# Contextual attention, two layers: half of the paste as fp16 products, three turning banks, chunks cut anew

## The chip, the cores and the metric

The kernel runs on one core of a Trainium2 chip. The metric is the device time of one execution in microseconds, lower is better; the number given is the median of three runs.

## The reference

Two equal layers, each over 4 images of 64 channels, 80 x 80, in fp32. For one image `b`:

```
f  = b[:, :, ::2, ::2]                                # 64 x 40 x 40
w  = 3x3 patches of f                                 # L = 1600 rows of 576
raw_w = 4x4 patches of b at stride 2                  # 1600 rows of 1024
wn = w / max(|w|, 1e-4)
y  = wn @ w.T * mm                                    # 1600 x 1600 scores
y  = softmax(10 * y, over the rows of wn) * mm
patches = y.T @ raw_w                                 # 1600 x 1024
out = patches added back where they overlap, / 4      # "paste", a transposed convolution
```

`mm` is 1 where the mask's 3x3 patch is all zero. Layer 2 takes layer 1's output. The 8 passes (2 layers x 4 images) are called units here.

## The kernel before, in words

The 40 x 40 points of `f` lie in 14 tiles of 123 (3 strips x 41). `G` holds the whole score matrix of a unit, 14 tiles of rows by 14 blocks of 123 columns. A unit goes through two stages, and the stages of two units lie side by side.

**Scores.** 28 score pairs (two tiles of rows each) in 4 column chunks (`S_CHUNKS`, start and width in blocks). PE's `score_tile` makes a tile's scores in `psG` (2 banks, one for each tile of a pair) with 14 fp16 matmuls over the split features `HL`, `LH`, `H1`, `HV` (L433); blocks that the symmetric matrix already holds are transposed out of `G` instead (fp32, L428), and then the first tile of the pair waits until ACT has copied all earlier tiles. DVE takes the scaled maximum (L723), ACT copies the scores to `G` (L565) and sums the exponentials (L575). At the end of a unit the log of the sum is made column by column (`lse_*`) and spread over rows by PE (`lse_row`, L362, into `psB`).

**Paste.** 28 paste pairs in 4 chunks (`P_CHUNKS`), each of two tiles. DVE turns scores into arguments (`argument_pair`, L773, one operand in PSUM), ACT takes the exponential (`softmax_pair`, L586), SP moves each tile down by one partition into `SH` (L270, four DMAs a pair), DVE adds it back (`add_shifted`, L784) and adds the neighbour tile into `Z` (`sum_pair`, L806, both operands in SBUF; `Z` has two slots of a pair). PE's `paste_tile` (L449) multiplies `Z` by the patch blocks `B` into `psO`, one bank for each of two column parities `b`; every fp32 matmul shows as two MATMUL records, so a tile has four. After 7 pairs ACT copies both banks out (`read_out`, L595) and SP stores them. The blocks `B` of the next unit are transposed by PE (`block_group`, L409) and copied by ACT (L549) one group a slot, in slots 21 to 27.

**The order** is written by hand. Each engine has a `body(u, v, w)`: unit `u` is pasted, `v` scored, `w` prepared, over slots `s` = 2 to 29; in a slot one pair of `u` is pasted and the score pairs of `score_list(s)` are made (PE: first score tile, first paste tile, second score tile, second paste tile). Slots 28 and 29 already paste chunk 0 of `v` and have no scores. `argument_pair` and `softmax_pair` run 4 slots ahead (`LEAD`), `add_shifted` 2 (`AHEAD`), `sum_pair` 1. In DVE's slot the order is argument, shifted add, sum, then scores; in ACT's: softmax, read_out (every 7 slots), scores, block group. At slot 24 `lse_row` of the first chunk stands on PE between the two halves. The body runs 9 times: once with scores alone, 7 times with both, once with paste alone. The features of the next unit are laid out by 8 DMAs on SP at slot 28 (L251), and POOL only copies a seam (`wrap`, L919, reads and writes `G`). Ahead of the first body DVE works out the mask and then `low_features(0)`, on which the first layout waits.

## Time and profile before

| | us |
|---|---|
| median of 3 runs | 1791.49 (1788.55 to 1794.37) |
| the profiled execution | 1782.45 |
| its span, first to last instruction | 1780.6 |
| PE, PE weight loads busy | 1591.8, 1052.2 |
| DVE, ACT, POOL busy | 1090.1, 901.4, 51.2 |
| mean granted TensorE clock | 0.952 |

The profile is of one execution. A busy time is the sum over an engine's instructions; matmuls overlap, so PE's real rate is read from the starts of successive groups, not from their lengths. In the rows below PE is the matmul engine, PEld its weight loads; "x9" is the number of instructions merged into a row, and the last bracket is the idle time ahead of it and what ended it. Busy times of a window stand in the order PE, PEld, DVE, ACT, POOL, then the granted clock.

### The profile page before, as it was taken

The numbers are of one execution on the slowest core, as the hardware profiler recorded it, in microseconds if no ns is written. First come the engines' busy times: TensorE is split into PE (matmuls) and PEld (weight loads), VectorE is DVE, ScalarE is ACT, GpSimd is POOL, SyncE is SP. The second block draws the span as 40 slices with busy tenths as digits, with TensorE's granted clock in tenths as the row PEclk, the third lists the DMA queues.
The fourth block names the chain that finished last, engine by engine and source line by source line (L and its number), as shares of the span: only waits on it lengthen the run. The fifth ranks groups of instructions, "written<-read, shape, count | busy, mean of one in ns | idle before, by whom it ended". The sixth has DMA issues, their size and how long they took to land.

```text
span 1780.6 us, 27285 instructions
## 1 busy us (share of the span) xinstructions
PE 1591.8 (89%) x7260; PEld 1052.2 (59%) x7260; DVE 1090.1 (61%) x2526; ACT 901.4 (51%) x2265; POOL 51.2 (3%) x62
## 2 busy tenths in 40 slices
PE   3887899998999899998999989999899989999986
PEld 3756566665666566565665656666566656656543
DVE  5224555675566756576656755667556676667784
ACT  1446454574446744565535645457344573457431
POOL 1000100001000000000000010000100000000100
PEclk9987899999999999998999999999889999999998
DMA  3400624226422445225352262422633234522342
GB/s 61 62 1 12 143 61 89 72 70 139 84 63 72 104 111 106 55 69 124 86 96 61 66 145 66 92 72 73 137 71 77 72 94 109 106 64 66 112 122 78
DMA packets 181701, 149.64 MB, mean 84 GB/s; under 512 B 120016, under 2 KB 177424, under 8 KB 181520
## 3 DMA queue, kind: packets, MB, share of 16 engines
q1 hardware_dynamic: 181522, 147.62, 35.1%
q8 instruction: 67, 1.10, 0.3%
q14 instruction: 112, 0.92, 0.2%
HBM read 19.78 MB, written 13.11 MB: 18 GB/s over the span
## 4 chain that ended last, share of the span: by engine, by line
PE 71%; DVE 10%; ACT 8%; issue 7%; SPq 2%; DMA 1%; DVEq 0%; ACTq 0%; POOL 0%; POOLq 0%
PE psG L433 35%; PE psO L449 30%; DVE S L723 4%; ACT S L575 3%; PE psG L428 3%; DVE G L773 2%; PE psM L347 2%; ACT G L565 2%; ACT OSB L595 1%; ACT G L586 1%; PE psB L362 1%; SPq L251 1%; DVE Z L806 1%; DVE G L784 1%; ACT SQ L529 1%
## 5 line engine op out<-in xcount | busy, mean ns | idle before, releaser
L449 PE MATMUL psO<-Z,B 123*128 123x492 f32 (+2 forms) x1792 | 786.5, 569 | 66.7 <-ACT OSB L595 57.9
L723 DVE CUSTOM_DVE_ANT_0 S<-psG,RB 123x369 f32<-123x369 f32 (+1 forms) x448 | 267.4, 605 | 547.3 <-PE psG L433 471.0
L565 ACT ACTIVATE G<-psG 123x369 f32<-123x369 f32 (+1 forms) x448 | 236.6, 529 | 695.8 <-DVE mx L723 693.9
L449 PEld LDWEIGHTS psO<-Z,B 123*128 123x128 f32 x1792 | 335.9, 199 | 301.3 <-issue 202.3
L433 PE MATMUL psG<-LH,HL 128*123 128x369 f16 (+3 forms) x2592 | 474.8, 329 | 26.2 <-issue 13.8
L433 PEld LDWEIGHTS psG<-LH,HL 128*123 128x123 f16 x2592 | 338.0, 138 | 175.3 <-issue 94.9
L586 ACT ACTIVATE G<-G,nb 123x492 f32<-123x492 f32 (+1 forms) x448 | 268.2, 646 | 125.5 <-DVE G L773 125.1
L575 ACT ACTIVATE S<-S,nm 123x360 f32<-123x360 f32 (+3 forms) x560 | 306.3, 551 | 0.1
L773 DVE SCALAR_TENSOR_TENSOR G<-G,RA,psB 123x492 f32<-123x492 f32 (+1 forms) x448 | 275.4, 658 | 21.8 <-issue 18.2
L784 DVE TENSOR_TENSOR G<-G,SH 123x492 f32<-123x492 f32 (+1 forms) x448 | 251.2, 601 | 14.7 <-DMA SH<-G 14.5
L806 DVE TENSOR_TENSOR Z<-G 123x984 f32<-123x984 f32 (+2 forms) x192 | 209.8, 1093 | 30.4 <-PE psO L449 30.3
L433 PE MATMUL psG<-H 128*123 128x369 f16 (+3 forms) x864 | 187.8, 327 | 0.0
L428 PEld LDWEIGHTS psG<-idn,G 123*123 123x123 f32 x688 | 103.8, 206 | 106.9 <-ACT G L565 81.9
L428 PE MATMUL psG<-idn,G 123*123 123x123 f32 x688 | 124.2, 302 | 43.0 <-ACT G L565 42.4
L433 PEld LDWEIGHTS psG<-H 128*123 128x123 f16 x864 | 114.3, 137 | 29.4 <-issue 0.9
L575 ACT ACTIVATION_READ_ACCUMULATOR S<-S,nm 123x1 f32 x560 | 106.6, 190 | 0.0
L433 PE MATMUL psG<-HV 128*123 128x369 f16 (+3 forms) x288 | 93.6, 325 | 0.0
L433 PE MATMUL psG<-HL 128*123 128x369 f16 (+3 forms) x288 | 93.4, 324 | 0.0
L919 POOL COPY G<-G 123x164 f32<-123x164 f32 x56 | 46.4, 828 | 1633.2 <-DVE Z L806 1143.1
L409 PEld LDWEIGHTS psM<-idn,XP 128*123 128x123 f32 x224 | 35.2, 200 | 18.5 <-issue 18.4
L433 PEld LDWEIGHTS psG<-HV 128*123 128x123 f16 x288 | 39.3, 136 | 9.7 <-issue 0.2
L433 PEld LDWEIGHTS psG<-HL 128*123 128x123 f16 x288 | 39.2, 136 | 9.6 <-issue 0.2
(74 smaller groups left out, 515.2 us busy)
## 6 DMA issues: line engine op xcount, KB each, us to landing
SH<-G SPq DMA_DIRECT2D x224, 214.8 KB
SH<-G SPq DMA_DIRECT2D x224, 161.0 KB
XP<-x SPq DMA_DIRECT2D x20, 280.0 KB, 5.5
XP<-mid SPq DMA_DIRECT2D x20, 280.0 KB, 5.4
SH<-G SPq DMA_DIRECT2D x224, 19.2 KB
HL<-SQ SPq DMA_DIRECT2D x16, 246.5 KB, 3.3
LH<-SQ SPq DMA_DIRECT2D x16, 246.5 KB, 4.5
SH<-G SPq DMA_DIRECT2D x224, 14.4 KB
```

What stands on the lines that cost most here:

```text
L347: last = pe.matmul(psM[0:TW, Q_BANK, r:r + 1], SQ[0:64, r * TW:(r + 1) * TW], ones[:, :], start=True, stop=True)
L428: last = pe.transpose(psG[0:TW, par, i * TW:(i + 1) * TW], G[:, c:c + TW], idn[0:TW, 0:TW])
L433: last = pe.matmul(psG[0:TW, par, stored_n * TW:w * TW], st[:, p:p + TW], mv[:, lo:lo + n], start=(i == 0), stop=(i == len(TERMS) - 1))
L449: last = pe.matmul(psO[:, b, 0:n], B[:, o:o + 128], Z[:, 2 * (s % 2) + j, 0:n], start=t == 0, stop=t == TILES - 1)
L565: act.activation(G[:, t * GLEN + c0:t * GLEN + c0 + n], psG[0:TW, par, 0:n], ACT.Copy).then_inc(g_read, 1)
L575: last = act.activation(y, y, ACT.Exp, bias=nm[:, k * TILES + t:k * TILES + t + 1], accum_out=sg[:, c:c + 1])
L586: act.activation(y, y, ACT.Exp, bias=nb[:, bass.ds(u * TILES + t, 1)]).then_inc(y_made, 1)
L723: dve.tensor_tensor_reduce(S[:, par, 0:n], psG[0:TW, par, 0:n], RB[:, s0 * TW:s0 * TW + n], 1.0, 0.0, ALU.mult, ALU.max, mx[:, par:par + 1 ...
L773: dve.scalar_tensor_tensor(out=g, in0=g, scalar=RA[:, bass.ds(u * TILES + t, 1)], in1=psB[0:TW, k % 2, 0:n], op0=ALU.mult, op1=ALU.subtrac ...
L784: dve.tensor_tensor(g, g, SH[:, o % SFREE, 0:n], ALU.add).then_inc(y1_made, 1)
L806: dve.tensor_tensor(Z[:, slot:slot + 2, 0:n], g[:, 2 * i:2 * i + 2, c0:c0 + n], g[:, 2 * i - 1:2 * i + 1, c0 - TW:c0 - TW + n], ALU.add).t ...
L919: pool.tensor_copy(g[:, :, GLEN - WRAP:GLEN], g[:, :, TW + PITCH:2 * TW]).then_inc(wrap_made, 1)
```

## The change

The even tile of a paste pair stays one fp32 product (`B` scaled by 4096). The odd tile becomes three fp16 products: `Z` is split in `Zh` (ACT, `high_pair`, scale 4096) and `Zl` (DVE, `low_pair`), the block in `Bh` (ACT) and `Bl` (DVE, `low_blocks`); PE forms `Bh Zh + Bl Zh + Bh Zl` for each parity. `psO` gets a third bank, `psM` loses one, and `O_BANK` turns the banks from chunk to chunk; only chunk 0 of a unit takes the banks that the last chunk of the unit before had. The chunks are cut anew, and scores start at slot 3. `add_shifted` moves from DVE to POOL and runs as soon as the shift has landed. DVE's slot is now low, sum, argument, low_blocks (slots 22 to 28), scores; ACT's is read_out, high, softmax, block group (a slot later than before), scores. The layout takes 6 DMAs, one of them a broadcast of three copies. The row spreads (`scale_rows`) stand one at the end of a body and three in slots 3 to 5, and `low_features(0)` stands ahead of the mask.

```diff
-P_CHUNKS = [(0, 4), (4, 4), (8, 3), (11, 3)]
-S_CHUNKS = [(0, 3), (3, 4), (7, 3), (10, 4)]
+P_CHUNKS = [(0, 3), (3, 4), (7, 4), (11, 3)]
+S_CHUNKS = [(0, 2), (2, 4), (6, 4), (10, 4)]
...
-    if s < 16:
-        return [s - FIRST]
-    if s < 21:
-        return [14, 15] if s == 16 else [s - 1]
-    if s < SLOTS:
-        return [20, 21] if s == 21 else [s]
-    return []
+    if s < 3 or s >= SLOTS:
+        return []
+    if s < 17:
+        return [s - 3]
+    if s < 22:
+        return [[14, 15], [16, 17], [18], [19], [20, 21]][s - 17]
+    return [s]
...
-        B = sb("B", [TW, TILES * 2 * 128], F32)
+
+        B = sb("B", [TW, PAIRS * 2 * 128], F32)
+        Bh = sb("Bh", [TW, PAIRS * 2 * 128], F16)
+        Bl = sb("Bl", [TW, PAIRS * 2 * 128], F16)
...
-        psO = ps("psO", [128, 2, 512])
+        psO = ps("psO", [128, 3, 512])
         psB = ps("psB", [128, 2, 512])
-        psM = ps("psM", [128, 2, 512])
+        psM = ps("psM", [128, 512])
...
+
...
-                for dst, src in ((HL[0:64, :], HS), (HL[64:128, :], LS), (LH[0:64, :], LS), (LH[64:128, :], HS),
-                                 (H1[0:64, :], HS), (H1[64:128, 0:n - 1], HS[:, 1:n]),
-                                 (HV[0:64, :], HS), (HV[64:128, 0:n - TW], HS[:, TW:n])):
+                for dst, src in ((PK[0:64, 0:3, :], HS.unsqueeze(1).to_broadcast([64, 3, n])), (HL[64:128, :], LS),
+                                 (LH[0:64, :], LS), (LH[64:128, :], HS),
+                                 (H1[64:128, 0:n - 1], HS[:, 1:n]), (HV[64:128, 0:n - TW], HS[:, TW:n])):
                     sp.dma_start(dst, src).then_inc(f_in, 16)
 
...
-                        pe.wait_ge(o_read, (u * NK + k + 1) * 2)
...
+                        pe.sem_inc(pe_gate, 1)
                         pe.wait_ge(b_made, u * PAIRS + i + 1)
+                else:
+                    pe.wait_ge(zl_made, u * SLOTS + k * PAIRS + i + 3)
                 for b in range(2):
-                    o = (2 * t + b) * 128
-                    last = pe.matmul(psO[:, b, 0:n], B[:, o:o + 128], Z[:, 2 * (s % 2) + j, 0:n],
-                                     start=t == 0, stop=t == TILES - 1)
+                    if t == 0:
+
+                        pe.sem_inc(pe_gate, 1)
+                        pe.wait_ge(o_read, (u * NK + k) * 2 + b + (2 if k == 0 else 1))
+                    o = (2 * i + b) * 128
+                    if j == 0:
+                        pe.matmul(psO[:, O_BANK[k][b], 0:n], B[:, o:o + 128], Z[:, 2 * (s % 2), 0:n],
+                                  start=t == 0, stop=False)
+                        continue
+                    for q, (w, z) in enumerate(((Bh, Zh), (Bl, Zh), (Bh, Zl))):
+                        last = pe.matmul(psO[:, O_BANK[k][b], 0:n], w[:, o:o + 128], z[:, s % 2, 0:n],
+                                         start=False, stop=t == TILES - 1 and q == 2)
                 if j == 1:
                     last.then_inc(z_used, 1)
...
+                act.activation(Bh[:, g * 256:(g + 1) * 256], psM[0:TW, 256:512], ACT.Copy).then_inc(bh_made, 1)
 
             def score_pair(u, v, j):
                 k, i = j // PAIRS, j % PAIRS
...
-                                   psO[:, b, 0:n].rearrange("p (s w) -> p s w", w=PITCH)[:, :, 0:HALF + 1],
-                                   ACT.Copy, scale=0.25).then_inc(o_read, 1)
+                                   psO[:, O_BANK[k][b], 0:n].rearrange("p (s w) -> p s w", w=PITCH)[:, :, 0:HALF + 1],
+                                   ACT.Copy, scale=0.25 / ZSCALE).then_inc(o_read, 1)
+
+            def high_pair(at, s):
+
+                u, k, i = at
+                n = p_cols(k, True)[1]
+                slot = s % 2
+                act.wait_ge(z_made, u * SLOTS + k * PAIRS + i + 2)
+                act.sem_inc(act_gate, 1)
+                act.wait_ge(z_used, u * SLOTS + k * PAIRS + i + 1)
+                act.activation(Zh[:, slot, 0:n], Z[:, 2 * slot + 1, 0:n], ACT.Copy, scale=ZSCALE).then_inc(zh_made, 1)
 
...
             def body(u, v, w):
                 for s in BODY:
-                    at = place(u, v, s + LEAD)
+                    if u is not None and s % PAIRS == 0 and s <= SLOTS:
+                        read_out(u, s // PAIRS - 1)
                     if s == 24 and v is not None:
                         lse_log(v, False)
-                    elif at:
+                    at = place(u, v, s + 1)
+                    if at:
+                        high_pair(at, s + 1)
+                    at = place(u, v, s + LEAD)
+                    if at and s != 24:
                         softmax_pair(at)
-                    if u is not None and s % PAIRS == 0 and s <= SLOTS:
-                        read_out(u, s // PAIRS - 1)
+                    if v is not None and (NK - 1) * PAIRS < s <= SLOTS:
...
-                            scale_rows(w, s - 25)
-                    if v is not None and (NK - 1) * PAIRS <= s < SLOTS:
-                        g = s - (NK - 1) * PAIRS
-                        block_group(u, v, g)
+                if w is not None:
+                    scale_rows(w, 0)
 
...
-            def add_shifted(at):
-                u, k, i = at
...
-                    dve.tensor_tensor(g, g, SH[:, o % SFREE, 0:n], ALU.add).then_inc(y1_made, 1)
...
+                dve.sem_inc(dve_gate, 1)
+                dve.wait_ge(zl_made, u * SLOTS + k * PAIRS + i + 1)
...
+            def low_pair(at, s):
+                u, k, i = at
+                n = p_cols(k, True)[1]
+                slot = s % 2
+                dve.wait_ge(zh_made, u * SLOTS + k * PAIRS + i + 1)
+                dve.scalar_tensor_tensor(out=Zl[:, slot, 0:n], in0=Z[:, 2 * slot + 1, 0:n], scalar=ZSCALE,
+                                         in1=Zh[:, slot, 0:n], op0=ALU.mult, op1=ALU.subtract).then_inc(zl_made, 1)
+
+            def low_blocks(v, g):
+                dve.wait_ge(bh_made, v * PAIRS + g + 1)
+                at = slice(g * 256, (g + 1) * 256)
+                dve.tensor_tensor(Bl[:, at], psM[0:TW, 256:512], Bh[:, at], ALU.subtract).then_inc(b_made, 1)
+
             def body(u, v, w):
                 for s in BODY:
-                    at = place(u, v, s + LEAD)
+                    at = place(u, v, s)
+                    if at:
+                        low_pair(at, s)
                     if s == 24 and v is not None:
                         lse_columns(v, False)
-                    elif at:
-                        if s == SLOTS + 1:
-                            lse_sum(v, True)
+                    if s == SLOTS + 1 and v is not None:
+                        lse_sum(v, True)
+                    at = place(u, v, s + 1)
+                    if at:
+                        sum_pair(at, s + 1)
+                    at = place(u, v, s + LEAD)
+                    if at and s != 24:
                         argument_pair(at)
-                    at_y = place(u, v, s + AHEAD)
-                    if at_y:
-                        add_shifted(at_y)
-                    at_z = place(u, v, s + 1)
-                    if at_z:
-                        sum_pair(at_z, s + 1)
                     if s == 23 and v is not None:
                         lse_max(v, False)
...
+            low_features(0)
...
-            low_features(0)
...
+            def add_shifted(at):
+                u, k, i = at
+                c0, n = p_cols(k)
+                for j, t in enumerate(arg_tiles(i)):
+                    o = k * TILES + 2 * i + j
+                    pool.wait_ge(sh_in[o % SFREE], (u * (NB // SFREE) + o // SFREE + 1) * 16 * len(SHIFT_PARTS))
+                    g = G[:, t * GLEN + c0:t * GLEN + c0 + n]
+                    pool.tensor_tensor(g, g, SH[:, o % SFREE, 0:n], ALU.add).then_inc(y1_made, 1)
...
                 for s in BODY:
+                    at = place(u, v, s + LEAD)
+                    if at:
```

## Rows read from the trace of the kernel before

**Rows 1.** The page: busy time of the engines, and the chain that ended last, by line.

```profile
PE 1591.8 (89%) x7260; PEld 1052.2 (59%) x7260; DVE 1090.1 (61%) x2526; ACT 901.4 (51%) x2265; POOL 51.2 (3%) x62
...
PE psG L433 35%; PE psO L449 30%; DVE S L723 4%; ACT S L575 3%; PE psG L428 3%; DVE G L773 2%; PE psM L347 2%; ACT G L565 2%; ACT OSB L595 1%; ACT G L586 1%; PE psB L362 1%; SPq L251 1%; DVE Z L806 1%; DVE G L784 1%; ACT SQ L529 1%
```

**Rows 2.** Timeline of PE in one slot: start us, length us, engine, instructions merged.

```profile
859.46 1.58 PE L433 MATMUL psG<-LH,HL 128*123 128x369 f16 x9
...
861.66 1.81 PE L449 MATMUL psO<-Z,B 123*128 123x492 f32 x4
863.31 1.58 PE L433 MATMUL psG<-LH,HL 128*123 128x369 f16 x9
```

**Rows 3.** Windows: the stretch with scores and paste, and the last body: busy us.

```profile
190.00:1666.00 1476.00, 1362.99 (x6290) 896.95 (x6288) 934.41 (x2177) 784.19 (x1986) 41.77 (x50) 0.96 0.37 88
...
1666.00:1773.00 107.00, 92.54 (x233) 45.56 (x234) 79.76 (x129) 30.75 (x55) 3.66 (x4) 0.92 0.40 111
```

**Rows 4.** Timeline of PE: first score tile, turn of an image, later chunk.

```profile
46.76 3.01 PE L433 MATMUL psG<-LH,HL 128*123 128x369 f16 x9 [4.38 <-DMA HV<-SQ]
...
620.38 8.56 PE L449 MATMUL psO<-Z,B 123*128 123x492 f32 x16 [3.89 <-ACT OSB L595]
...
632.16 1.62 PE L433 MATMUL psG<-LH,HL 128*123 128x369 f16 x9 [2.80 <-issue]
...
675.93 3.40 PE L449 MATMUL psO<-Z,B 123*128 123x492 f32 x4 [3.02 <-ACT OSB L595]
```

**Rows 5.** Waits of PE from 200 to 1660: total us, times, longest.

```profile
PE psO L449 <- ACT OSB L595: 47.5, 20, 3.9
PE psG L428 <- ACT G L565: 22.4, 35, 1.6
PE psB L362 <- DVE lse L761: 15.8, 7, 2.3
```

**Rows 6.** Window after the wait at 672.9: busy us of PE, PEld, DVE, ACT, POOL; PEclk.

```profile
675.80:679.00 3.20, 3.07 (x4) 1.41 (x5) 0.58 (x3) 0.56 (x2) 0.00 (x0) 0.51 0.42 126
```

**Rows 7.** Timeline of ACT in slot 22 (transposes only).

```profile
785.49 0.55 ACT L575 ACTIVATE S<-S,nm 123x320 f32<-123x320 f32 x1
...
787.26 0.58 ACT L549 ACTIVATE B<-psM 123x512 f32<-123x512 f32 x1
787.74 1.09 ACT L586 ACTIVATE G<-G,nb 123x369 f32<-123x369 f32 x2
788.73 1.17 ACT L565 ACTIVATE G<-psG 123x492 f32<-123x492 f32 x2
```

**Rows 8.** Timelines of DVE and of PE (four transposes, then paste) in the same slot.

```profile
787.01 1.09 DVE L806 TENSOR_TENSOR Z<-G 123x902 f32<-123x902 f32 x1
788.02 0.66 DVE L723 CUSTOM_DVE_ANT_0 S<-psG,RB 123x492 f32<-123x492 f32 x1
...
785.76 0.59 PE L428 MATMUL psG<-idn,G 123*123 123x123 f32 x4
786.19 1.68 PE L449 MATMUL psO<-Z,B 123*128 123x451 f32 x4
```

**Rows 9.** Groups by form: the operation nearest to the new one on DVE.

```profile
L773 DVE SCALAR_TENSOR_TENSOR G<-G,RA,psB 123x492 f32<-123x492 f32 x224 | 151.9, 723 | 19.8 <-issue 17.2 <-ACT G L565 2.1
```

**Rows 10.** Timeline of POOL and of DVE at the same times; POOL memsets by form.

```profile
603.51 0.33 POOL L919 COPY G<-G 123x164 f32<-123x164 f32 x1 [164.62 <-DVE Z L806]
...
618.23 1.11 POOL L919 COPY G<-G 123x164 f32<-123x164 f32 x1 [6.71 <-DVE G L784]
...
617.98 1.18 DVE L806 TENSOR_TENSOR Z<-G 123x984 f32<-123x984 f32 x1
...
L905 POOL MEMSET XP<- 128x3444 f32 x1 | 3.0, 2967 | 0.3 <-POOLq L941 0.3
...
L906 POOL MEMSET SQ<- 128x1972 f32 x1 | 1.7, 1741 | 0.0
```

**Rows 11.** Timeline of PE in the last body.

```profile
1750.82 23.07 PE L449 MATMUL psO<-Z,B 123*128 123x451 f32 x56 [7.02 <-ACT OSB L595]
```

More of the change, by code:

```diff
@@ L33 @@
 BIG = 1.0e30
+ZSCALE = 4096.0
 FREE = 2
@@ L343, in row_squares @@
                 if v is not None:
-                    pe.wait_ge(r_rows, v * 4 + 3)
+                    pe.wait_ge(r_rows, v * 4 + 4)
                 for r in range(FROWS):
-                    last = pe.matmul(psM[0:TW, Q_BANK, r:r + 1], SQ[0:64, r * TW:(r + 1) * TW], ones[:, :],
+                    last = pe.matmul(psM[0:TW, r:r + 1], SQ[0:64, r * TW:(r + 1) * TW], ones[:, :],
                                      start=True, stop=True)
@@ L352, in band_sums @@
                 pe.wait_ge(r_step, w * R_STEPS + 3)
-                if v is not None:
-                    pe.sem_inc(pe_gate, 1)
-                    pe.wait_ge(r_rows, v * 4 + 4)
-                pe.matmul(psM[0:TW, BAND_BANK, 0:TILES], band[:, :], qv[:, :],
+                pe.matmul(psM[0:TW, 0:TILES], band[:, :], qv[:, :],
                           start=True, stop=True).then_inc(norm_cols, 1)
@@ L395, in block_group @@
                     pe.sem_inc(pe_gate, 1)
-                if g < 2 and w is not None:
-                    pe.wait_ge(r_step, w * R_STEPS + (1 if g == 0 else 4))
-                elif g < 2:
-                    pe.wait_ge(r_rows, v * 4 + 3 + g)
-                elif g < 5:
-                    pe.wait_ge(b_made, v * PAIRS + g - 1)
+                if g > 0:
+                    pe.wait_ge(b_made, v * PAIRS + g)
+                elif w is not None:
+                    pe.wait_ge(r_step, w * R_STEPS + 4)
                 else:
-                    pe.wait_ge(b_made, v * PAIRS + g)
+                    pe.wait_ge(r_rows, v * 4 + 4)
                 for t in (2 * g, 2 * g + 1):
@@ L457, in body @@
                     pairs = score_list(s) if v is not None else []
-                    if s == 4 and v is not None:
-                        scale_rows(u, v, 2)
-                        scale_rows(u, v, 3)
+                    if 3 <= s <= 5 and v is not None:
+                        scale_rows(u, v, s - 2)
                     if s == 5 and u is not None:
@@ L464, in body @@
                         lse_row(u, 3)
-                    if s == FIRST and v is not None:
+                    if pairs and pairs[0] == 0:
                         pe.wait_ge(f_in, (v + 1) * N_F * 16)
@@ L482, in body @@
                         block_group(v, w, s - 21)
-                    if w is not None and s in (25, 26):
-                        scale_rows(v, w, s - 25)
+                if w is not None:
+                    scale_rows(v, w, 0)
                 if v is not None:
@@ L489, in _ @@
             for t in range(TILES):
-                last = pe.matmul(psM[0:TW, 0, 2 * t:2 * t + 2], G[0:LAYERS, MASK_AT + t * TW:MASK_AT + (t + 1) * TW],
+                last = pe.matmul(psM[0:TW, 2 * t:2 * t + 2], G[0:LAYERS, MASK_AT + t * TW:MASK_AT + (t + 1) * TW],
                                  idn[0:LAYERS, 0:LAYERS], start=True, stop=True)
@@ L633, in body @@
                         softmax_pair(at)
-                    if s == 4 and v is not None:
-                        scale_rows(v, 2)
-                        scale_rows(v, 3)
+                    if v is not None and 3 <= s <= 5:
+                        scale_rows(v, s - 2)
                     if w is not None:
@@ L665, in _ @@
         def _(dve):
-            for tile, value in ((HL[:, :].bitcast(F32), 0.0), (LH[:, :].bitcast(F32), 0.0), (H1[:, :].bitcast(F32), 0.0),
-                                (HV[:, :].bitcast(F32), 0.0), (ones[:, :], 1.0), (SH[:, :, :], 0.0), (SHJ[:, :], 0.0)):
+            for tile, value in ((PK[:, :, :].bitcast(F32), 0.0), (ones[:, :], 1.0), (SH[:, :, :], 0.0), (SHJ[:, :], 0.0)):
                 dve.memset(tile, value).then_inc(cleared, 1)
             dve.sem_inc(z_made, 1)
-            dve.sem_inc(y1_made, SFREE)
+            dve.sem_inc(zl_made, 2)
             def low_features(w):
@@ L827, in body @@
                         lse_max(v, True)
+                    if v is not None and (NK - 1) * PAIRS < s <= SLOTS:
+                        low_blocks(v, s - 1 - (NK - 1) * PAIRS)
                     if s == SLOTS + 1 and v is not None:
```

66 lines of the change are left out of this document (29 added, 37 removed).

## Prediction

> **What bounds the kernel now.** I read the page first: PE is busy 1591.8 of 1780.6 us, and the chain that ended last runs over PE's scores and paste for 65% of the span, with small pieces of DVE and ACT [rows 1]. So PE's own work comes first, its waits second. The timeline of PE in a slot without waits gives the rates: 14 score matmuls of 369 columns take 861.66 - 859.46 = 2.20 us, 0.426 ns a column; the four records of a 492-column paste tile take 1.65 us, 0.84 ns a column [rows 2]. fp32 paste thus costs twice per record, and has two records a product. The windows then show where this rules: from 190 to 1666 us, seven units of 210.9 us with scores and paste side by side, PE is busy 92% and DVE 63%; in the last body, paste alone, it is 86% and 75% [rows 3]. Third come the places where PE stands still: up to 3.9 us for the copy-out of `psO` when a chunk turns, then 2.8 us at the loop's edge with no releaser shown [rows 4], and in total 47.5 us for the copy-out, 22.4 us for copied scores ahead of transposes and 15.8 us for the log-sum row [rows 5]. After the 3.02 us wait the granted clock is 0.51 for some 3 us, that is TensorE at 1.2 in place of 2.4 GHz, and a tile of scores or paste takes twice as long [rows 4, 6]; so a wait of that length costs about 1.6 us more than itself. Last I looked where PE does not rule: in slots 22 to 25 nearly all scores are transposes (0.1 us each) and PE's slot is down to some 4.3 us with its eight paste records of 451 columns, and ACT has 4.3 us as well, end to end: exponentials from 785.49 to 787.26, block, softmax, two copies up to 789.8 [rows 7, 8].
>
> **The change part by part.**
>
> *Paste, odd tiles.* Per column of an odd tile four records at 0.84 ns (3.35 ns) give way to six fp16 ones at 0.426 ns (2.56 ns), 0.80 ns saved. A unit has 7 odd tiles in each chunk, and the chunks' columns add up to 1804: 12,628 columns, 10.1 us. It counts in the seven units where PE rules: **-70.7 us**. A 128-wide fp16 weight load is shown under 157 ns matmuls today, and 205 ns ones cover it better.
>
> *New chunks of the scores.* Counting `score_tile` over the new chunks, blocks made by matmul go from 110 to 112 a unit (14 x 123 x 0.426 ns = 0.73 us each), transposes from 86 to 84 (0.43 / 4 = 0.1 us each [rows 8]): +1.3 us for eight units, **+10.4 us**. Pairs whose first tile is partly transposed, and so waits for all copies, fall from 16 to 12, but the cover for that wait, the odd tile, falls from 1.65 to 1.26 us. I leave the 22.4 us [rows 5] as they are outside the short slots.
>
> *Third bank, copy-out a slot later.* At three of four turns the waits go: 47.5 us less 7 x 3.9 us at the turn of a unit leaves 20 us [rows 4, 5]. At a unit's turn the banks are the old ones, yet the first waits for one copy only and `read_out` no longer stands behind a softmax pair: 1.3 us each, 9 us, since DVE and ACT are late next. **-29 us**. With the turns of 3 us one slow stretch a unit goes, 1.5 us each by [rows 6]: **-10 us**.
>
> *Added on ACT and DVE.* `high_pair`: nearest are the softmax activations, SBUF to SBUF, 0.5 us for 369 columns from start to start [rows 7]; on 451 columns 0.55. `low_pair`: the 492-column three-operand form, 0.72 us [rows 9], here 0.57. Blocks: two copies of 256 for one of 512, +0.07 on ACT; `low_blocks` some 0.35 on DVE. DVE sheds the two shifted adds. In a slot of 7 us all of this is hidden under PE. In slots 22 and 23 it isn't, and there is a new order: DVE's `low_blocks`, which waits for ACT's block copy, which stands behind the softmax, now stands ahead of the two maxima, on which ACT's copies and then PE's transposes wait. Counted from the last maximum of a slot: copy and exponentials 2.35 [rows 7], high 0.55, softmax 0.99, block copies 0.55, `low_blocks` 0.35, two maxima with hops 1.3 [rows 8]: 6.1 us where 4.3 stand today. Two slots, +3.6 us. In 24 and 25 today's 15 us hold the log-sum wait and a slow stretch already; I take them as unchanged, and so take back the 1.5 us of paste credited to the four slots. 4.9 x 7: **+34 us**. Bounds: 0, if the four slots' slack hides it, and 68.
>
> *Shifted adds on POOL.* The trace has no such add. POOL's memsets give 0.833 ns a column and 0.1 us: 0.51 us for 492 columns is the low end; the copy of 164 columns took 0.33 us, 2.0 ns a column, and with two inputs of 492 that makes 1.98 us, the high end [rows 10]. Twice the memset's rate is 0.92 us; I take 1.1, nearer to the low end, as the copy is of short runs. The GPSIMD Engine Reference of the Trainium skill, in Performance versus the Vector engine, gives 4497 ns for an fp32 add of 2048 columns; by that an estimate is 1.08 us, and the sum would not move. Two adds a pair, 2.2 us, are hidden in any slot. What isn't: the POOL copy that started at 618.23, while DVE's sum of two SBUF operands ran to 619.16, took 1.11 us, and the one at 603.51, beside no such operation, 0.33 [rows 10]. So the two kinds shut each other out, and DVE keeps two such operations a slot (sum and `low_pair`). The Trainium skill, SBUF - State Buffer, Who interferes with whom, states it as an exclusive lock for a whole instruction, held against either side; the trace shows POOL blocked, not yet DVE. With POOL busy 2.2 of 6.1 us a DVE operation meets it about one time in three and waits 0.55: 0.4 us a slot, which counts in the 28 short slots: **+11 us**. Bounds 0 and 62 (both wait a whole add).
>
> *Start and end.* `low_features(0)` ahead of the mask frees the layout on which the first score tile waited 4.38 us [rows 4], but the mask comes later: **-2 us**. Last body: DVE had argument, two adds and a sum, 3.8 us for a pair; now POOL's adds and DVE's two locked operations add up to 2 x 1.1 + 1.6 = 3.8. Only part of the 7.0 us copy-out wait [rows 11] and the like goes: **-6 us**; bounds +20 and -25. Layout in six DMAs: no term, the releaser of the 2.8 us at the edge isn't a DMA, and scores start a slot later.
>
> Sum: -70.7 + 10.4 - 29 - 10 + 34 + 11 - 2 - 6 = -62. On the profiled execution, 1782.45, that is 1720; on the median, 1791.5, it is **1729**, which I give.
>
> **The rivals.**
>
> A. *The alternation of ACT and DVE costs in 24 and 25 too* (3.6 x 7 = 25 us): 1754. For it: ACT is full in 22 and 23 already. Against: PE's own waits hide it there. Chance 0.17.
>
> B. *POOL holds up DVE, slower.* Place: the short slots and the last body. If an add takes `a` and both of DVE's locked operations wait a whole one, the short slots cost 56a and the last body 24 x (2a + 1.6 - 3.8); with all else as above the change is -120 + 104a, which turns slower at a = 1.15 us. At the high end, 1.98, it is +86: 1877. For it: the locked copy of [rows 10] took more than three times its length. Against: whole waits each time need an unlucky phase, and POOL runs ahead by three slots. Chance 0.10.
>
> C. *The short slots hold and the last body follows PE* (2.63 us a pair): 34 and 19 us more gain, 1676. Chance 0.12.
>
> D. *No change to speak of*: A, and three more slots that lose 1.8 us each where the third chunk's scores are transposed (+38): 1792. Chance 0.05.
>
> My forecast has 0.56. Two runs of this kernel can be told apart from about 0.3%, 5 us. Faster: forecast, A and C, 0.85; same: D, 0.05; slower: B, 0.10. The range takes in both bounds of the short slots and A, and leaves out B and the edge of C: 1680 to 1783.
>
> **What would show it.** Right, step by step: odd tiles of 492 columns in 1.26 us; PE's wait for the copy-out only at a unit's turn, some 15 to 20 us in all; fewer stretches at 0.5 clock; a period of about 6 us in slots 22 and 23, with DVE waiting for ACT's block copy; POOL adds near 1.1 us, some stretched, some `low_pair` and sums longer than 0.6 and 1.2 us; a unit in 203 us (210.9 less 7.9). Wrong: POOL adds over 1.5 us with DVE's sums stretched in most slots (B); PE waiting for `Zl` in the long slots, which would mean that the splitting is late everywhere; fp16 paste matmuls over 0.22 us.

## The result, and the profile after

The change makes the kernel slower: 1855.17 us (median of 4 runs, 1853.24 to 1864.79) against 1790.02 for the kernel before, run beside it, ratio 1.0388, 95% interval 1.0345 to 1.0431. Forecast was 1729, at most 1783.

The page of after, busy times and the chain that ended last by engine, answers to [rows 1]:

```profile
PE 1575.0 (85%) x7916; PEld 1034.5 (56%) x7916; DVE 1093.2 (59%) x2355; ACT 1034.2 (56%) x2545; POOL 547.1 (29%) x510
...
PE 51%; ACT 14%; issue 12%; DVE 11%; SPq 6%; DMA 4%; POOL 1%; ACTq 1%; DVEq 0%; POOLq 0%
```

No engine became the bound: PE is down from 89% to 85%, DVE's busy time is what it was, ACT is at 56%, POOL at 29%. PE is 51% of the chain, where its scores and paste alone were 65%; ACT and "issue" have come up. So the time went into waiting on each other.

The windows of after, first paste to last body and the last body (us, then PE, PEld, DVE, ACT, POOL busy; granted clock), answer to [rows 3]:

```profile
198.80:1725.00 1526.20, 1338.47 (x6870) 880.55 (x6868) 936.10 (x2027) 899.65 (x2228) 476.55 (x443) 0.95 0.36 85
1725.00:1856.00 131.00, 97.96 (x291) 42.88 (x291) 82.83 (x108) 48.77 (x87) 60.44 (x55) 0.83 0.34 95
```

A unit takes 1526.2 / 7 = 218.0 us where 203 was forecast and 210.9 stood before. The last body takes 131 us against 107, with the clock at 0.83, and the first paste is at 198.8 against 190.2. Over the span: 8.6 + 50.4 + 23.4 = 82.4 us, the whole of 1863.0 - 1780.6. The medians are 65 us apart and not 82: the profiled execution of after (1864.79 us) was the longest of its four, that of before one of its shorter ones.

To see what PE does with its time I split it from the start of each matmul to the start of the next: **own work** (columns x 0.417 ns + 2.5 ns, twice per column for an fp32 record, at least 105 ns for one; that is 156 and 208 ns for fp16 columns of 369 and 492 and 413 ns for an fp32 record of 492 at full clock, where [rows 2] and after show 157, 208 and 412), what a low granted clock adds, and the rest, in which it stands **still**:

| us, seven units | own work | low clock | still | sum |
|---|---|---|---|---|
| before | 1280.3 | 46.6 | 149.0 | 1475.9 |
| after | 1217.5 | 69.2 | 239.6 | 1526.3 |
| after, last body (before: 85.4, 5.9, 15.9) | 75.3 | 17.1 | 38.4 | 130.8 |

PE's own work fell by 62.8 us, as the forecast had it (7/8 of 10.4 less 70.7 is -61.6). It stands still 90.6 us more, and the low clock costs 22.6 more in place of 10 less. The question is who makes it wait. Its waits in that stretch answer to [rows 5]:

```profile
PE psG L423 <- ACT G L569: 58.1, 60, 7.0
PE psM L362 <- ACT RB L544: 26.4, 14, 3.3
PE psO L450 <- issue: 22.7, 5, 4.9
PE psB L362 <- DVE lse L774: 21.8, 14, 2.4
PE psO L450 <- ACT OSB L599: 20.2, 12, 2.2
PE psG L428 <- ACT G L569: 17.9, 27, 1.6
PE psM L404 <- DVE Bl L826: 15.2, 17, 1.5
...
PE psO L454 <- DVE Zl L820: 1.6, 1, 1.6
```

The copy-out costs 20.2 us where it cost 47.5 (the forecast said 15 to 20, at a unit's turn alone: six of the twelve waits stand there, 2.2 us each, and six at the turn from chunk 0 to chunk 1, 1.2 us each), and PE hardly ever waits for `Zl`. But transposes wait 58.1 us for ACT's copies (22.4 before), and 26.4 us are a wait that hardly existed: the row spreads (`scale_rows`, L362) for ACT's copy of the one before, as `psM` now has a single bank. Waits of the weight loads are apart in this view; where there were two kinds, I compare slots by their starts.

Timeline of PE in slots 21 to 23, which answers to [rows 8]:

```profile
807.76 0.35 PE L454 MATMUL psO<-Zh,Bh 123*128 123x451 f16 x1
...
808.90 0.62 PE L404 MATMUL psM<-idn,XP 128*123 128x128 f32 x4
809.74 0.69 PE L423 MATMUL psG<-idn,G 123*123 123x123 f32 x4 [0.22 <-ACT G L569]
...
813.96 0.72 PE L404 MATMUL psM<-idn,XP 128*123 128x128 f32 x4 [0.44 <-DVE Bl L826]
815.78 0.69 PE L423 MATMUL psG<-idn,G 123*123 123x123 f32 x4 [1.09 <-ACT G L569]
...
822.24 0.84 PE L423 MATMUL psG<-idn,G 123*123 123x123 f32 x4 [1.09 <-ACT G L569]
```

An odd tile of 451 columns takes 808.90 - 807.76 = 1.14 us, six products 0.19 apart; at 492 columns they are 0.208 apart, 1.25 us. The short slots run at a period of 6.0 and 6.5 us (809.74, 815.78, 822.24), with PE waiting for ACT's copies and for `Bl`: the mechanism and the 6.1 us of the forecast.

Timeline of PE at three other places of the next unit:

```profile
868.95 2.82 PE L450 MATMUL psO<-Z,B 123*128 123x369 f32 x4 [4.93 <-issue]
...
880.91 0.69 PE L362 MATMUL psM<-idn,R 123*123 123x123 f32 x4 [1.55 <-ACT RB L544]
...
888.30 0.48 PE L362 MATMUL psM<-idn,R 123*123 123x123 f32 x2 [1.55 <-ACT RB L544]
```

The first is the loop's edge, 4.93 us where [rows 4] showed 2.80; its four records of 369 columns then take 2.82 us, where four of 492 take 1.81 at full clock [rows 2]. The other two are spreads: ACT's copy of a row stands behind that slot's scores in ACT's order.

DVE, POOL and SP where a shift is late (a new place, in slot 11):

```profile
708.81 13.25 SPq L274 DMA_DIRECT2D SH<-G  x10
...
715.53 1.22 POOL L939 TENSOR_TENSOR G<-G,SH 123x492 f32<-123x492 f32 x1 [14.71 <-DMA SH<-G]
...
717.09 2.15 DVE L812 TENSOR_TENSOR Z<-G 123x984 f32<-123x984 f32 x1 [4.74 <-POOL G L939]
719.15 1.35 DVE L786 SCALAR_TENSOR_TENSOR G<-G,RA,psB 123x492 f32<-123x492 f32 x2
719.35 0.61 ACT L611 ACTIVATE Zh<-Z 123x492 f16<-123x492 f32 x1 [5.82 <-DVE Z L812]
```

The shift itself was late, as SP had twelve stores and loads to issue ahead of it, from 697.65 to 708.70 us, and POOL waited 14.71 us for the landing. DVE waited 4.74 us for POOL's add, and behind that wait, on DVE, stood the argument (L786) and all scores; ACT waited 5.82 us for the same sum, with its softmax and scores behind. The experiments ask how much of the loss has this pattern.

### The profile page after: what moved, and what is told of

Read it like the earlier page. It is cut to its first block, busy times and chain, and to the rows that moved or that the text cites. A ratio compares the mean times of both kernels' runs of the same rounds, so it can differ in the third digit from the quotient of the medians.

```text
span 1863.0 us, 29803 instructions
## 1 busy us (share of the span) xinstructions
PE 1575.0 (85%) x7916; PEld 1034.5 (56%) x7916; DVE 1093.2 (59%) x2355; ACT 1034.2 (56%) x2545; POOL 547.1 (29%) x510
## 4 chain that ended last, share of the span: by engine, by line
PE 51%; ACT 14%; issue 12%; DVE 11%; SPq 6%; DMA 4%; POOL 1%; ACTq 1%; DVEq 0%; POOLq 0%
PE psG L428 31%; PE psO L450 11%; ACT S L579 6%; PE psO L454 5%; DVE S L736 4%; DMA SH<-G 3%; SPq L274 2%; ACT G L569 2%; ACT G L590 2%; DVE G L786 2%; DVE Z L812 2%; SPq L219 2%; SPq L262 2%; PE psG L423 1%; POOL G L939 1%
## 5 line engine op out<-in xcount | busy, mean ns | idle before, releaser
L939 POOL TENSOR_TENSOR G<-G,SH 123x492 f32<-123x492 f32 (+1 forms) x448 | 517.8, 1161 | 1301.1 <-DMA SH<-G 1299.9
L428 PE MATMUL psG<-PK 128*123 128x492 f16 (+1 forms) x4256 | 727.7, 325 | 21.6 <-ACT G L569 21.6
L428 PEld LDWEIGHTS psG<-PK 128*123 128x123 f16 x4256 | 532.4, 139 | 222.4 <-issue 48.1
L736 DVE CUSTOM_DVE_ANT_0 S<-psG,RB 123x492 f32<-123x492 f32 (+1 forms) x448 | 266.0, 603 | 460.6 <-PE psG L428 425.1
L450 PE MATMUL psO<-Z,B 123*128 123x492 f32 (+2 forms) x896 | 425.6, 600 | 75.1 <-ACT OSB L599 23.7
L569 ACT ACTIVATE G<-psG 123x492 f32<-123x492 f32 (+1 forms) x448 | 233.1, 525 | 453.8 <-DVE mx L736 451.6
L579 ACT ACTIVATE S<-S,nm 123x480 f32<-123x480 f32 (+3 forms) x560 | 307.0, 552 | 9.4 <-DVE nm L740 8.7
L786 DVE SCALAR_TENSOR_TENSOR G<-G,RA,psB 123x492 f32<-123x492 f32 (+1 forms) x448 | 274.9, 654 | 1.3 <-issue 1.1
L454 PE MATMUL psO<-Zh,Bh 123*128 123x492 f16 (+2 forms) x448 | 168.4, 376 | 3.2 <-DVE Zl L820 3.2
L454 PE MATMUL psO<-Zh,Bl 123*128 123x492 f16 (+2 forms) x448 | 167.0, 373 | 0.0
L454 PE MATMUL psO<-Zl,Bh 123*128 123x492 f16 (+2 forms) x448 | 166.5, 372 | 0.0
```

Source lines behind the costliest of these rows:

```text
L428: last = pe.matmul(psG[0:TW, par, stored_n * TW:w * TW], st[:, p:p + TW], mv[:, lo:lo + n], start=(i == 0), stop=(i == len(TERMS) - 1))
L450: pe.matmul(psO[:, O_BANK[k][b], 0:n], B[:, o:o + 128], Z[:, 2 * (s % 2), 0:n], start=t == 0, stop=False)
L454: last = pe.matmul(psO[:, O_BANK[k][b], 0:n], w[:, o:o + 128], z[:, s % 2, 0:n], start=False, stop=t == TILES - 1 and q == 2)
L569: act.activation(G[:, t * GLEN + c0:t * GLEN + c0 + n], psG[0:TW, par, 0:n], ACT.Copy).then_inc(g_read, 1)
L579: last = act.activation(y, y, ACT.Exp, bias=nm[:, k * TILES + t:k * TILES + t + 1], accum_out=sg[:, c:c + 1])
L736: dve.tensor_tensor_reduce(S[:, par, 0:n], psG[0:TW, par, 0:n], RB[:, s0 * TW:s0 * TW + n], 1.0, 0.0, ALU.mult, ALU.max, mx[:, par:par + 1 ...
```

## The experiments

All are edits of the kernel after, in five groups (e1 to e4, e5 to e8, e9 to e12, e13 to e15, e16), so an expectation knows the results of the groups ahead of it. Ratios are to the kernel before, run beside each group. Where two kernels are compared below, the difference is that of their ratios x 1790 us; by the intervals of the two ratios it is good to some 10 us either way (3 to 12). In the diffs, cut to their core, `at1`, `at2`, `at4` are the pairs 1, 2 and 4 slots ahead.

| run | us | ratio (95%) |
|---|---|---|
| after | 1855.2 | 1.039 (1.035 to 1.043) |
| e1 adds on DVE, argument first | 1961.2 | 1.098 (1.094 to 1.102) |
| e2 adds on DVE, sum first | 1887.7 | 1.057 (1.054 to 1.061) |
| e3 `low_blocks` behind the maxima | 1824.9 | 1.021 (1.016 to 1.025) |
| e4 row copies ahead of the scores | 1839.6 | 1.031 (1.027 to 1.035) |
| e5 shifts ahead of SP's stores and loads | 1867.5 | 1.045 (1.040 to 1.049) |
| e6 no split, fp32 | 1814.2 | 1.016 (1.011 to 1.021) |
| e7 argument and softmax first | 1818.8 | 1.019 (1.013 to 1.024) |
| e8 e3, e4 and e5 | 1816.2 | 1.018 (1.013 to 1.023) |
| e9 e3, e4 and e7 | 1755.5 | 0.982 (0.980 to 0.984) |
| e10 e9, spreads moved off the edge | 1760.8 | 0.985 (0.982 to 0.987) |
| e11 fp32, e4, e7, spreads as e10 | 1724.3 | 0.966 (0.963 to 0.970) |
| e12 fp32, adds on DVE, order of before | 1785.5 | 1.000 (0.998 to 1.002) |
| e13 products, no splitting | 1775.7 | 0.994 (0.991 to 0.997) |
| e14 splitting, no products | 1890.9 | 1.061 (1.057 to 1.064) |
| e15 fp32, e4, e7 | 1733.2 | 0.972 (0.968 to 0.975) |
| e16 e15 with the products, no splitting | 1697.8 | 0.947 (0.943 to 0.952) |

**Is it POOL?** e1 and e2 put the shifted add back on DVE, ahead of the sum; e1 also puts DVE's argument first. ACT's order stays that of after in both.

```diff
 DVE's slot, e1:
     low_pair(at, s)
+    argument_pair(at4)
+    add_shifted(at2)
     sum_pair(at1, s + 1)
-    argument_pair(at4)
```

> The shifted add goes back to DVE, with the order of before (low, argument, add, sum). Theory P (late adds: POOL's add is longer, stands behind DVE's two-operand operations and stretches them, and DVE's sum now comes before the argument, so that each pair gets through later): the 67 us that DVE waited for POOL and most of the 38 us of stalls of the last body go, 1855 falls by 50 to 80 us, to 1775 to 1805, and the last body from 131 us to below 115. Rival Q (the new order around the block copies and the single psM bank make the stalls, DVE has no room for the adds): the time stays within 15 us of 1855 or rises, since DVE's slot grows by 1.25 us.

> Only the engine of the shifted add is undone; DVE keeps sum ahead of argument (low, add, sum, argument). If the engine is what matters in theory P, this is as fast as the variant with the old order within 10 us. If it is the order (argument late, two slots from argument to add are too short), it stays near 1855 and the last body near 130 us, while the variant with the old order gains. Rival Q: no gain in either.

Both are slower than after. So with the split in place, POOL's adds help, and rival B, as it was put, is not the cause. e1 is the worst of all, which I read as argument, two adds and a sum all standing ahead of what ACT's `high_pair` waits for. The traces fit that reading: from 203 to 1690 us ACT's wait for DVE's sum ahead of `Zh` is 393 us in e1, 275 in e2 and 195 in after. No run isolates it, and the adds on DVE with both engines in the order of before (as in e7) were not run with the split in place.

**Short slots and rows.**

```diff
 DVE's slot, e3:
-    low_blocks(v, s - 22)
     for j in score_list(s): score_pair(v, j)
+    low_blocks(v, s - 22)
 ACT's slot, e4:
+    if 3 <= s <= 5: scale_rows(v, s - 2)
     for j in score_list(s): score_pair(u, v, j)
-    if 3 <= s <= 5: scale_rows(v, s - 2)
```

> low_blocks stands behind the score maxima in DVE's slot, all else as after. Theory of the prediction (the block copy ahead of the maxima makes slots 22 and 23 6.1 us long): they fall to about 5 us, slots 22 to 27 give back 1 to 2 us each, 7 units, 25 to 50 us in all: 1805 to 1830. Rival: ACT is full there anyway, the wait moves to PE's block transposes, less than 10 us.

> ACT copies the spread rows (slots 3 to 5) ahead of its scores and not behind them, all else as after. If PE's two waits of 1.55 us a unit for the single psM bank are real cost, 3.1 us x 7 plus some slow clock goes: 20 to 30 us, to 1825 to 1835. Rival: PE waits there for something else that is late as well (the loop's edge, late sums), under 8 us.

e3 gives back 32 us: the place and the size of the forecast's +34. Timeline of PE in e3, slots 22 and 23:

```profile
791.00 1.68 PE L450 MATMUL psO<-Z,B 123*128 123x451 f32 x4
...
796.52 1.68 PE L450 MATMUL psO<-Z,B 123*128 123x451 f32 x4
...
801.22 1.68 PE L450 MATMUL psO<-Z,B 123*128 123x451 f32 x4
...
808.75 1.72 PE L450 MATMUL psO<-Z,B 123*128 123x451 f32 x2
```

Slot 22 is down to 801.22 - 796.52 = 4.7 us; slot 23, with its log-sum wait, to 7.5 here and 7.3 in the mean of seven (9.1 after). e4 gives 14 us. The wait for the spread in e4 from 199 to 1700 us, 26.4 us in 14 times in after:

```profile
PE psM L362 <- ACT RB L544: 5.7, 3, 2.1
```

Slots 3 and 4 fell from 8.2 and 8.3 us to 6.4 each. The forecast had no term for this.

**The late shift, and the split as a whole.**

```diff
 SP's slot, e5:
+    shift_pair(at4)
     stores and loads
-    shift_pair(at4)
 PE, e6 (high_pair, low_pair and low_blocks go too):
-    for q, (w, z) in enumerate(((Bh, Zh), (Bl, Zh), (Bh, Zl))):
-        last = pe.matmul(...)
+    last = pe.matmul(psO[:, O_BANK[k][b], 0:n], B[:, o:o + 128], Z[:, 2 * (s % 2) + j, 0:n], ...)
```

> SP issues the shift of a pair ahead of the feature and image loads of its slot, all else as after. If the wait of DVE's sum for POOL's add in slot 11 (2.8 us of stall a unit, behind 12 stores and loads on SP's queue) is real cost, the slot falls from 10.8 to 8 us: 20 us less, to 1830 to 1840. Rival: the wait only moves to the image or to the next store, under 8 us.

> Both tiles of a pair in fp32 again: high_pair, low_pair, low_blocks and the waits on them are left out, the block copy is one of 512; third bank, chunks, spread rows and POOL's adds stay as after. Theory S (the split gives less on PE than its order takes away): PE's own work rises by 81 us, yet the stalls of slots 21 to 27, of the last body and of the double pairs go, so the time is 1835 to 1865, the same as after within 20 us: the split as built is worth nothing. Rival T (the split pays, other parts of the change cost): the time rises by 60 to 80 us, to over 1910.

e5 is a miss: slot 11 fell from 10.8 to 8.1 us, but slots 29 and 2, around the loop's edge, rose from 8.6 and 6.6 to 9.6 and 8.6, and the whole gained nothing (11 us slower, within the noise of the two ratios). e6 shows two things at once: the whole split costs 40 us, and the rest of the change, without it, is 29 us slower than before where some 26 us of gain were forecast.

**The order.** e7 puts back what before had: argument ahead of the sum on DVE, softmax ahead of `high_pair` on ACT.

```diff
 DVE's slot, e7:
     low_pair(at, s)
+    argument_pair(at4)
     sum_pair(at1, s + 1)
-    argument_pair(at4)
 ACT's slot, e7:
+    softmax_pair(at4)
     high_pair(at1, s + 1)
-    softmax_pair(at4)
```

> Adds on POOL as after, but DVE does the argument ahead of the sum and ACT the softmax ahead of high_pair. Theory P in its part on latency (from argument to add there are two slots, in the last body too short at 2.9 us): the last body falls from 131 to about 115 us, the time by 15 to 25 us. Rival: the high half comes later on ACT and low_pair with it, as in the run with adds on DVE in that order; then the time rises, by 20 us or more.

> low_blocks behind the maxima, spread rows copied ahead of the scores, and the shift first on SP, together. If the three stalls are of different places their gains add up: -30 and -15 as measured, and -20 for the shift: 1785 to 1800, level with the kernel before. If they hide behind one another, above 1805.

e7 gives back 36 us, 14 of them in the last body (131 to 116). Waits of e7 over its seven units (202 to 1693 us), where after shows 196.9 and 62.9 us (95 and 15 times):

```profile
ACT Zh L611 <- DVE Z L812: 80.2, 91, 8.4
DVE Z L812 <- POOL G L939: 33.6, 14, 7.6
```

Nothing was made faster; what waits for POOL now stands behind what others wait for. e8, with the failed e5 in it, is worth 37 us, no more than e3 and e4 by themselves (46; the 9 between them are within the noise).

**Putting it together.** e9 is e3, e4 and e7. e10 also takes the two spreads that stand at the end of the body into slot 2. e11 is e10 without the split. e12 is e6 with the adds on DVE and the order of before.

```diff
 PE's body, e10 and e11:
     paste_tile(at, s, j)
+    if s == 2: lse_row(u, 1); scale_rows(u, v, 0)
...
-    scale_rows(v, w, 0)
-    lse_row(v, 1)
 DVE's slot, e12:
+    argument_pair(at4); add_shifted(at2); sum_pair(at1, s + 1)
-    sum_pair(at1, s + 1); argument_pair(at4)
```

> Three orders mended together, no part of the change undone: argument and softmax ahead of sum and high half, low_blocks behind the maxima, spread rows copied ahead of the scores. Theory O (the loss is one of order, at places that are apart): the single gains of 36, 30 and 15 us add up, 1855 falls to 1765 to 1785, below the kernel before. Rival: they hide behind one another as with the shift on SP, 1800 or more.

> As the mended order, and the last two spreads of a body (row scale and log-sum row) move behind the first paste pair of the next one. Theory E (PE's 4.9 us at the loop's edge, 2.8 before, is the sequencer's fetch, hidden before by two pairs of queued paste, and laid open since PE now waits for the log-sum row just ahead of the branch): PE's idle time at the edge falls by 1.5 to 3 us in each of 5 repeats, with the wait for the row 0.8 to 2 us a unit goes: 10 to 25 us below the run with the mended order. Rival: the edge costs what it costs on all engines, under 5 us.

> The same mends without the split: both tiles fp32, third bank, POOL adds, argument ahead of sum, rows early, spreads behind the edge. With the fp32 paste in the order of after at 1814, rows early should give 15, the argument first 15, the edge 10: 1770 to 1790. Compared with the run above it says what the split is worth once the order is mended: PE's own work says 70 us for the split; if ACT and DVE stay in its way, less than 20.

> Both tiles fp32 and the adds on DVE in the order of before: what is left of the change is third bank, chunks, spread rows, layout and start. If the third bank brings what was forecast and the row waits take it back, this is level with before, 1780 to 1800. If POOL's adds were what slows the fp32 variant (1814), it is below 1790; if POOL's adds help it, above 1814.

The three orders together give 102 us, at least the 32 + 14 + 36 = 82 that they give one by one (the 20 between them are no more than the noise of four ratios), and turn the change into a gain of 1.8%. Moving the spreads off the edge gives nothing with the split (e10, +5). e11, the page:

```profile
PE 1572.2 (91%) x7468; PEld 1034.6 (60%) x7468; DVE 918.0 (53%) x2075; ACT 903.2 (52%) x2265; POOL 514.4 (30%) x510
...
PE 69%; ACT 7%; issue 6%; DVE 6%; SPq 6%; DMA 4%; POOL 1%; ACTq 0%; DVEq 0%; POOLq 0%
```

At 1724 us it is the fastest kernel of the study that computes everything, and it has no fp16 product in the paste at all. e12 equals before: third bank, new chunks, layout, start and the new places of the row spreads are worth nothing together. There the copy-out has lost most of its waits (16.6 us left of 47.5), and others have come. PE's waits in e12, units two to eight:

```profile
PE psO L443 <- issue: 24.6, 5, 5.4
PE psM L358 <- ACT RB L533: 18.3, 14, 1.9
...
PE psO L443 <- ACT OSB L587: 16.6, 12, 1.8
```

**Gain and cost of the split apart.** e13 multiplies three fp16 products from buffers that are set to zero once; it leaves out the splitting, and with it the odd tiles' contribution to the paste. e14 does all of the splitting, and PE waits for it but multiplies fp32. e15 is e11 without the moved spreads. e16 has e15's order and e13's products, and leaves out the same part of the paste.

```diff
 ACT and DVE, e13 and e16:
-    high_pair(at1, s + 1)
-    low_pair(at, s)
-    low_blocks(v, s - 22)
 PE, e14:
-    for q, (w, z) in enumerate(((Bh, Zh), (Bl, Zh), (Bh, Zl))):
-        last = pe.matmul(psO[:, O_BANK[k][b], 0:n], w[:, o:o + 128], z[:, s % 2, 0:n], ...)
+    last = pe.matmul(psO[:, O_BANK[k][b], 0:n], B[:, o:o + 128], Z[:, 2 * (s % 2) + j, 0:n], ...)
```

> After with the three fp16 products but without the work of splitting: Zh, Zl, Bh and Bl are set once to zero and high_pair, low_pair, low_blocks and the copy of Bh are left out, so the odd tiles contribute nothing. Theory S (the products pay on PE, the splitting takes it all back): against the fp32 paste in the same order, 1814, this falls by 40 to 75 us, to 1740 to 1775. Rival (the products save nothing because PE's waits grow by as much, whatever fills ACT and DVE): 1795 to 1815.

> After with all of the splitting and its waits, but PE multiplies both tiles in fp32 and the block copy is of 512 columns. Theory S: against 1814 the splitting costs 70 us or more, 1880 to 1930, that is slower than after. Rival (the splitting is hidden where PE has more work): 1815 to 1850, faster than after or level.

> The fp32 mended version with the two spreads back at the end of the body. With the split, moving them cost 5 us in place of gaining 10 to 25; if the same holds here, 1715 to 1725; if the move is what helped the fp32 version, 1735 or more. Either should be below both kernels.

> Leaves out the odd tiles' contribution to the paste: their three fp16 products are multiplied from buffers set to zero once, and nothing is split. The order is that of the run with fp32 in both tiles, argument ahead of sum and the row copies early (1733 us, ratio 0.972). In the order of after the same products were worth only 38 us of the 71 that PE's own work lost. Theory: the other 33 went into waits for DVE and ACT that the order of after makes, and comes out once the order is mended: 1733 - 65 to 71, 1662 to 1668, ratio near 0.933. Rival: the time that PE saves goes to engines that have no slack whatever their order, so the gain stays near 38: 1695, ratio near 0.950. The run with the split in mended order (1755) then gives what the splitting costs there: 90 us by the first, 60 by the second.

From e6 the products give -39, the splitting costs +79, and both +40; the two add up. In the mended order the products give -44 (e15 to e16), the splitting +62 (e16 to e9). The medians themselves are 35 and 58 us apart; the rest comes from before, which took 1792 us beside e16 and 1786 to 1787 beside the others. So 39 and 44 can't be told apart. The page of e13 and of e14, busy times:

```profile
PE 1540.8 (87%) x7916; PEld 1021.8 (58%) x7916; DVE 918.8 (52%) x2079; ACT 894.2 (50%) x2265; POOL 528.3 (30%) x510
```

```profile
PE 1629.4 (86%) x7468; PEld 1057.2 (56%) x7468; DVE 1096.5 (58%) x2355; ACT 1046.6 (55%) x2545; POOL 546.0 (29%) x510
```

e14 has 178 us more on DVE than e13, and 152 more on ACT. Neither reaches 60%, which speaks against their throughput and for the chains in which each stands with the others in the slots where PE is short; that is argued from the shares and the slots, and no run isolates it. The three orders don't remove this cost. Of the 61 us between the traces of e16 and e9, slots 21 to 28 hold 34 and the last body 15, and in e9 PE's block transposes wait for the `Bl` of the group before, as `psM` is a single bank (PE's waits in e9 from 188 to 1618 us):

```profile
PE psM L404 <- DVE Bl L826: 29.0, 41, 2.0
```

In e16 they wait 2.4 us. A second `psM` bank for them was not tried.

Why do the products give 39 or 44 and not 71? By the account, from e15 to e16 own work falls by 72.7 us, low clock costs 6.6 more, and standing still 34.0 more. By slot (mean of seven units), standing still grows by 0.4 to 0.6 us in slots 16, 17, 18, 21, 23, 25 and 27, by 0.2 in 22, 24 and 26, by 0.8 and 0.9 in 6 and 11, each against 0.3 to 0.4 saved: there the odd tile was the cover of ACT's copy or of DVE's maximum, not the bound. PE's waits in e15 and e16, units two to eight, show it in one line each:

```profile
PE psG L419 <- ACT G L557: 8.3, 15, 1.0
PE psG L424 <- ACT G L557: 7.1, 9, 1.8
```

```profile
PE psG L423 <- ACT G L566: 23.1, 43, 4.0
...
PE psG L428 <- ACT G L566: 13.8, 15, 4.7
```

Waits for copied scores rise from 15.4 to 36.9 us. The first theory of that run (the mended order frees all 71) fell; the rival, 1695, was right within 3 us.

## Why the prediction was wrong

The sum was -62 us and the result is +65 (+69 by the ratio). The runs cut the difference into steps:

| step | runs | forecast | measured |
|---|---|---|---|
| chunks, third bank, low clock, start | before to e12 | 10.4 - 29 - 10 - 2 = -31 | 0 |
| adds on POOL, sum ahead of argument, last body | e12 to e6 | 11 - 6 = +5 | +30 |
| splitting | e6 to e14 | +34 | +79 |
| fp16 products | e14 to after | -71 | -39 |
| sum | | -62 | +69 |

All four steps failed by 25 to 45 us, in one direction. The second also changes DVE's order, so its 30 us are not those of the adds alone.

- **Fp16 products, "It counts in the seven units where PE rules".** This step failed. The rates were right to a tenth: 1.25 us a tile, own work down 72.7 us (70.7). But "PE is busy 92%" was taken as "PE rules in every slot". In twelve of 28 slots (e15 to e16) the saved 0.4 us, half of it, or, in slots 6 and 11, more than it came back as a wait. The forecast had even named the mechanism ("the cover for that wait, the odd tile, falls from 1.65 to 1.26 us") and then priced it at nothing.
- **Splitting, "In a slot of 7 us all of this is hidden under PE".** This step failed most. The term of 34 us for `low_blocks` was right (e3: 32; slot 22 at 6.1 us as worked out). The other 45 lie elsewhere: from e6 to e14 slots 22 and 23 lose 4.2 us a unit, which is the term; slots 17, 24 and 25, the latter two taken "as unchanged", lose 3.9 (27 us), the last body 7.5, the start 3.3, and some 9 us are spread over other slots (the two traces are 76 us apart). Of all this 16 us are low clock. The sum had `low_blocks` standing ahead of the maxima, but not PE's next block transposes waiting for it, 29.0 us in e9 where it stands behind them.
- **Adds on POOL.** The size of an add was right: taken 1.1 us, measured 1.29 on 492 columns and 1.03 on 369 in the mean (rows in the last section), blocking included; those that met no DVE instruction took 0.83 to 0.97 us on 369 columns and 1.05 to 1.23 on 492. By the turning point that the forecast gave rival B, 1.15 us, these adds stand right at it, and the change still isn't slower because of POOL: the same kernel with the adds on DVE is slower yet (e2, in the order of after). The forecast priced the lock and forgot the order. DVE's sum now waits for another engine, with the argument behind it. In fp32, argument first and rows early, e15 against e6, are worth 79 us with the same adds on POOL, and e15 is 50 us ahead of e12, which has the adds on DVE and the rows late. Slots 3 and 4, where the rows stand, hold 23 of these 50, so in this order the adds on POOL gain and don't cost; no run has them changed alone in it.
- **Third bank and copy-out.** -29 was right for its own waits: 47.5 to 20.2 us, -27. What failed is that nothing was put against it for the `psM` bank it was paid with. In e12 slots 3 and 4 stand still 1.6 and 1.7 us each, 3.2 x 7 = 22 us more than before, with 18.3 us of waits for the row copy in that stretch, and the loop's edge has grown.
- **Chunks.** +9.1 us forecast for the seven units, some 9 to 10 measured (own work of e12 less before's). The term was right.
- **Low clock, -10.** With fp32 and the adds on DVE it is -8.1 (e12); with all of the change +22.6. It rises and falls with the time that PE stands still, from 23 us (e11) to 98 (e1), while the term had been set alone.
- **Start, -2, and last body, -6.** They came as +8.6 and +23.4. The slots of the last body take 2.9 us each at 492 columns where all is in time, but the way of a pair (argument, exponential, four DMA issues, landing, POOL, DVE, ACT) is one chain there; e7's order gives 14 of the 23 us back, and fp32 with that order is down to 104.6 us (e15), below before's 107.
- **The rivals.** A came true in part: from e6 to e14 slots 24 and 25 lose 2.5 us a unit, 17 us of its 25. So did D's place, slots that lose where the third chunk is transposed (slots 17 and 18). C did not: slot 22 took its 6.1 us and the last body grew. None had the case that happened: an order that puts cross-engine waits ahead of everybody's work. Ten in a hundred for "slower" was too little for a change that gives three engines new hand-overs in every slot.

## What to carry to other kernels

A busy share of 92% over a stretch doesn't say that the engine rules in each of its slots: take a saving per slot, and only where the slot shows no wait that the saved work was covering. In an in-order engine, whatever waits for another engine goes behind everything that others wait for; here the three moves that follow it were worth 102 us, more than the arithmetic that the change was about. Measure gain and cost of such a trade apart (e13 and e14 did it in two runs), and try the rest of the change without it: the best kernel here is the one without the split.

## What the runs showed of the hardware

The forecast had seen POOL held up by DVE, not DVE by POOL. The runs show both. Groups by form, in after:

```profile
L939 POOL TENSOR_TENSOR G<-G,SH 123x492 f32<-123x492 f32 x224 | 287.5, 1292 | 497.4 <-DMA SH<-G 496.4
L939 POOL TENSOR_TENSOR G<-G,SH 123x369 f32<-123x369 f32 x224 | 230.3, 1031 | 803.7 <-DMA SH<-G 803.5
...
L812 DVE TENSOR_TENSOR Z<-G 123x984 f32<-123x984 f32 x96 | 145.8, 1519 | 55.0 <-POOL G L939 49.6 <-PE psO L454 5.1
...
L740 DVE TENSOR_SCALAR nm<-mx 123x2 f32<-123x2 f32 x224 | 61.2, 273 | 7.8
```

The same in e12, adds on DVE:

```profile
L805 DVE TENSOR_TENSOR Z<-G 123x984 f32<-123x984 f32 x96 | 112.8, 1175 | 0.0
...
L726 DVE TENSOR_SCALAR nm<-mx 123x2 f32<-123x2 f32 x224 | 37.9, 169 | 7.8
```

And both sides meeting in the last body, POOL and DVE in after:

```profile
1798.14 1.22 POOL L939 TENSOR_TENSOR G<-G,SH 123x492 f32<-123x492 f32 x1 [0.46 <-DMA SH<-G]
1798.15 2.25 DVE L812 TENSOR_TENSOR Z<-G 123x984 f32<-123x984 f32 x1 [2.46 <-PE psO L454]
1799.54 1.95 POOL L939 TENSOR_TENSOR G<-G,SH 123x492 f32<-123x492 f32 x1 [0.17 <-DMA SH<-G]
```

DVE's sum ended 1.04 us after POOL's add, near its own undisturbed length, so it was stretched to 2.25 us; then POOL's next add took 1.95. What I had not expected is the last row of each group: an operation on two columns with one tensor input grows from 169 to 273 ns in the mean. The mean hides two kinds: in after the 152 that met no POOL instruction took 169 ns, as all 224 do in e12, and the 72 that met one took 493 ns in the mean and up to 1145. The Trainium skill (SBUF — State Buffer, Who interferes with whom) has the port pair held for a whole instruction by DVE operations in a 2-port mode too, and not only by those with two SBUF inputs; the trace agrees in that this operation is held up, and whether it runs in such a mode isn't shown.

At the loop's edge, which comes five times, PE stood still 2.5 to 3.1 us before; in after it was 4.2 to 4.9, and up to 4.2 in e9 and 6.8 in e15, without a releaser in the trace. Moving two spreads off it was worth 10 us in fp32 (e11 against e15, edge waits 11.0 us in all against 30.5), and nothing with the split (e10 against e9): there the edge gave only 3 us (18.2 to 15.2), and PE's wait for the row copies rose from 2.7 to 13.9. What the edge's time is made of stays open.
